# Reordering the steps of two state-space layers and an attention layer of one fused Trainium2 program

## The chip, the core and the metric

The program runs on one core of one Trainium2 chip. Five engines work side by side, each on its own queue and in the order of that queue: PE (TensorE, matrix products and transposes), DVE (VectorE), ACT (ScalarE), POOL (GpSimd) and SP (SyncE, which only issues transfers). They meet at semaphores alone. The metric is the time of one execution in device microseconds; the median of three runs counts.

## The reference, cut to what matters

Four layers follow each other on x of 8 sequences x 512 tokens x 256 features, all in float32: linear attention (layer 0), a state-space layer (layer 1), softmax attention with 16 heads (layer 2), and a second state-space layer (layer 3) whose tokens are permuted on the way in and back on the way out. All are modulated by a condition vector. A state-space layer computes, for one sequence:

```
h   = layernorm(x) * (1 + scale) + shift
xm, z = split(h @ W_in)                      # 512 channels each
u   = silu(causal_conv4(xm) + conv_b)
dtr, B, C = split(u @ W_x)                   # 64, 16, 16
dt  = softplus(dtr @ W_dt + b_dt)
s_t = s_{t-1} * exp(dt_t * A) + (dt_t * u_t) * B_t     # 512 x 16 states
y_t = sum_n s_t[:, n] * C_t[n] + u_t * D
out = x + gate * ((y * silu(z)) @ W_out)
```

The attention layer projects q, k and v, takes a softmax over 512 keys per head, normalises the result, and adds silu(...) @ W_out to its input.

## The kernel before, in words

**State-space layers (`mamba`, lines 579 to 1165).** The batch entry (one sequence) is the outer loop, `batches`: b = 0 alone, then a hardware loop of three turns over two batches each, then b = 7 alone. Inside a batch there are 64 units, `s = 4 n + j` for the state n (16) and the block j of 128 channels (4). For each unit

- ACT makes `dA = exp(dt * A)` (L837) into a ring of 8, and `dub`, the tokens of `dt * u` scaled by B, for the next n (L823), into two buffers;
- PE turns `dub` over into `ps_dbu` (L1150), a ring of 3 banks in PSUM;
- DVE scans along the tokens (L946, `TENSOR_TENSOR_SCAN`), which gives the state h;
- POOL multiplies h by C (L1012), and PE sums over n into `ps_y`: for odd n, DVE first adds two neighbours (L912, for three of four blocks, three units later), then PE adds the sum with an identity (L1137; L1133 and L1134 for the fourth block). The first such sum of each block also takes `u * D` (L1123). PE runs the sums seven units late.

Between the units stand the steps that prepare batch b + 1 (`prep_step` on each engine, by unit number): layer norm (statistics L867 and L872 on DVE, reciprocal root L752 on ACT, shift L877 on DVE, application L759 on ACT), turning (L1041), the eight input projections (L1052, four for xm, then four for z) whose results ACT copies out of the one PSUM bank `misc` (L769, L776), the convolution (L884 and three times L888 for each block), the two silus (L780, L782, with a load of their function table ahead and one behind), `u @ W_x` (L1062), and the softplus in pieces (L793 to L802, summed on DVE at L899). The steps that finish batch b - 1 (`post_step`, `out_proj`) stand there too. In layer 3, POOL gathers the rows of x by index for batch b + 1 ahead of unit 0 (L975, four DMAs) and the rows of the output of b - 1 ahead of unit 59 (L992, four DMAs), and adds them to the residual in one piece at unit 63 (L997).

**Attention layer (`softmax_attention`, lines 1184 to 1757).** A batch has 32 steps i. In each, PE writes two score matmuls for the exponentials (L1700) and two for the row maxima of work further ahead (L1693) into a ring of four banks; ACT takes the exponentials (L1579), DVE the maxima (L1414). Half of the steps also hold `times_v` (L1676). After eight steps the result of four heads is copied (L1421, `products_out`), turned (L1685, `turn`) and divided (L1431, `quotient`). The layer norms, q, k and v of later batches and the output projection of the batch before share two banks: `ps_x` for turning x, q, k (L1635) and v (L1643), `ps_o` for turning y (L1660) and the output (L1639, L1643). `take` makes PE wait until the last reader of a bank is through.

## Time and profile before

| | us |
|---|---|
| median of three runs (lowest, highest) | 3574.3 (3567.9, 3591.2) |
| the profiled execution, time | 3575.5 |
| its span | 3573.8 |
| busy in the span: PE, DVE, ACT, POOL | 2743.9 (77%), 2574.5 (72%), 2177.2 (61%), 1662.6 (47%) |
| layer 1: first scan to last | 438.1 to 1485.8 |
| layer 2: first exponential to last | 1620.9 to 2303.9 |
| layer 3: first scan to last | 2414.2 to 3526.5 |

A row of the profile names an engine, the line of the kernel, the operation and the tiles it writes and reads. Its time is the length of one instruction, or of several in a row where it ends in xN. Where the row has brackets, the engine stood idle before it for that long, and the name in them is what it waited for last. PEclk is TensorE's granted clock as a share of 2.4 GHz. Busy shares over the whole span mix four layers with different limits, so the windows of single batches tell more.

### The profile page before, as it was taken

The numbers are of one execution on the slowest core, as the hardware profiler recorded it, in microseconds if no ns is written. First come the engines' busy times: TensorE is split into PE (matmuls) and PEld (weight loads), VectorE is DVE, ScalarE is ACT, GpSimd is POOL, SyncE is SP. The second block draws the span as 40 slices with busy tenths as digits, with TensorE's granted clock in tenths as the row PEclk, the third lists the DMA queues.
The fourth block names the chain that finished last, engine by engine and source line by source line (L and its number), as shares of the span: only waits on it lengthen the run. The fifth ranks groups of instructions, "written<-read, shape, count | busy, mean of one in ns | idle before, by whom it ended". The sixth has DMA issues, their size and how long they took to land. (4 is left out here: it accounts for less than half of the span.)

```text
span 3573.8 us, 39139 instructions
## 1 busy us (share of the span) xinstructions
PE 2743.9 (77%) x11156; PEld 1451.4 (41%) x11156; DVE 2574.5 (72%) x3375; ACT 2177.2 (61%) x3550; POOL 1662.6 (47%) x1213
## 2 busy tenths in 40 slices
PE   5887487888878878748888888748787787877875
PEld 4555244445444445412333333214443444434443
DVE  2443288888888889767766677528888878888795
ACT  0333477877877878414554555537776776767773
POOL 0000167867767768720000000016776767768685
PEclk8899699999999999868988899968998899988998
DMA  2010101101111011143444444010101202111021
GB/s 85 24 35 18 63 24 49 54 26 56 39 41 56 31 49 49 49 78 52 70 66 73 72 72 66 19 63 25 49 32 48 68 25 67 37 55 55 25 72 43
DMA packets 104219, 176.92 MB, mean 50 GB/s; under 512 B 10741, under 2 KB 91421, under 8 KB 95166
## 3 DMA queue, kind: packets, MB, share of 16 engines
q1 hardware_dynamic: 99775, 161.69, 17.3%
q0 software_dynamic: 4224, 12.59, 1.0%
q8 instruction: 102, 1.67, 0.2%
q14 instruction: 118, 0.97, 0.1%
HBM read 139.70 MB, written 34.14 MB: 49 GB/s over the span
## 5 line engine op out<-in xcount | busy, mean ns | idle before, releaser
L1012 POOL TENSOR_TENSOR l_h<-l_h,l_c_all 128x512 f32<-128x512 f32 x1024 | 1437.7, 1420 | 559.0 <-DVE l_h L946 539.5
L946 DVE TENSOR_TENSOR_SCAN l_h<-l_dA,l_ps_dbu 128x512 f32<-128x512 f32 x1024 | 1211.6, 1207 | 307.6 <-PE l_ps_dbu L1150 167.3
L823 ACT ACTIVATE l_dub<-l_duT,l_b_tok 128x512 f32<-128x512 f32 x1024 | 725.8, 713 | 244.0 <-PE l_ps_dbu L1150 243.7
L1150 PE MATMUL l_ps_dbu<-ident,l_dub 128*128 128x128 f32 x4096 | 634.3, 289 | 264.2 <-DVE l_h L946 183.0
L1150 PEld LDWEIGHTS l_ps_dbu<-ident,l_dub 128*128 128x128 f32 x4096 | 495.1, 147 | 706.9 <-DVE l_h L946 388.3
L837 ACT ACTIVATE l_dA<-l_dt,l_a_neg 128x512 f32<-128x512 f32 x1024 | 727.9, 713 | 0.2
L1137 PE MATMUL l_ps_y<-l_h,ident 128*128 128x512 f32 x768 | 457.8, 682 | 81.7 <-DVE l_h L912 80.9
L1414 DVE TENSOR_REDUCE l_q_max<-l_ring 128x1 f32<-128x512 f32 x512 | 327.4, 683 | 192.9 <-PE l_ring L1693 191.6
L1579 ACT ACTIVATE l_probs<-l_ring 128x512 f32<-128x512 f32 x512 | 282.7, 596 | 300.7 <-PE l_ring L1700 298.9
L975 POOL DMA_INDIRECT l_x_in<-x_dram,l_idx_x x32 | 31.3, 978 | 805.7 <-DMA l_idx<-in_idx 792.6
L912 DVE TENSOR_TENSOR l_h<-l_h 128x512 f32<-128x512 f32 x384 | 351.5, 919 | 23.3 <-POOL l_h L1012 22.8
L1052 PE MATMUL l_misc<-l_modT,l_w_in 128*128 128x512 f32 x512 | 260.5, 634 | 20.2 <-ACT l_modT L764 9.5
L1693 PE MATMUL l_ring<-l_ks,l_qs 99*128 99x512 bf16 x512 | 216.4, 425 | 24.9 <-DVE l_q_max L1414 21.3
L1700 PE MATMUL l_ring<-l_qs,l_ks 102*128 102x512 bf16 x512 | 208.1, 411 | 18.2 <-DMA l_qs<-l_m_parts 6.4
L1137 PEld LDWEIGHTS l_ps_y<-l_h,ident 128*128 128x128 f32 x768 | 138.9, 214 | 189.9 <-DVE l_h L912 117.1
L888 DVE SCALAR_TENSOR_TENSOR l_work<-l_conv_in,vecs,l_work 128x512 f32<-128x512 f32 x192 | 181.7, 946 | 6.8
L979 POOL TENSOR_TENSOR l_conv_in<-l_dt,l_u 128x512 f32<-128x512 f32 x64 | 81.5, 1273 | 138.9 <-DVE l_dt L899 138.9
L1676 PE MATMUL l_ps_y<-l_probs,l_v 128*32 128x512 f32 x1024 | 143.0, 634 | 1.0 <-ACT l_probs L1579 1.0
L321 POOL DMA_DIRECT2D x_dram<-l_res x8 | 6.3, 786 | 293.2 <-DVE l_res L366 293.2
L1103 PE MATMUL l_misc<-l_w_out,l_y 128*128 128x256 f32 x512 | 120.8, 390 | 26.4 <-DVE l_og L919 24.9
L1052 PEld LDWEIGHTS l_misc<-l_modT,l_w_in 128*128 128x128 f32 x512 | 94.4, 205 | 109.0 <-issue 68.7
L1133 PE MATMUL l_ps_y<-l_h,ident 128*128 128x512 f32 x256 | 131.3, 595 | 0.0
(202 smaller groups left out, 3097.0 us busy)
## 6 DMA issues: line engine op xcount, KB each, us to landing
l_c_all<-c_rows_dram SPq DMA_DIRECT2D x64, 1024.0 KB, 4.7
l_res<-x_dram SPq DMA_DIRECT2D x24, 512.0 KB, 6.4
parts_dram<-l_parts SPq DMA_DIRECT2D x48, 256.0 KB, 2.7
l_qs<-parts_dram SPq DMA_DIRECT2D x48, 256.0 KB
l_ks<-parts_dram SPq DMA_DIRECT2D x48, 256.0 KB
l_x_in<-x_dram SPq DMA_DIRECT2D x16, 512.0 KB, 5.4
x_dram<-l_res SPq DMA_DIRECT2D x16, 512.0 KB, 3.2
su_cond_w<-in_cond_w SPq DMA_DIRECT2D x1, 5120.0 KB, 14.8
```

The lines of the kernel that those rows point to most:

```text
L823: return act.activation(dub[:, n % 2, t, :], duT[:, p, t, :], ACT.Copy, scale=b_tok[:, p, t, n:n + 1])
L837: act.activation(dA[:, s % DA_RING, :], dt[:, p, j, :], ACT.Exp, scale=a_neg[:, j * N + n:j * N + n + 1]).then_inc(da_ok, 1)
L912: dve.tensor_tensor(h[:, h_slot(s0), :], h[:, h_slot(s0), :], h[:, h_slot(s), :], ALU.add).then_inc(add_ok, 1)
L946: dve.tensor_tensor_scan(h[:, h_slot(s), :], dA[:, s % DA_RING, :], ps_dbu[:, dbu_slot(s), :], 0.0, ALU.mult, ALU.add).then_inc(scan_ok, 1)
L1012: pool.tensor_tensor(h[:, h_slot(s), :], h[:, h_slot(s), :], c_all[:, (n // C_GROUP) % 2, n % C_GROUP, :], ALU.mult).then_inc(hc_ok, 1)
L1052: last = pe.matmul(misc[:], w_in[:, k, e * P:(e + 1) * P], modT[:, k, :], start=(k == 0), stop=(k == DH - 1))
L1137: pe.matmul(ps_y[:, j, :], ident[:], h[:, h_slot(s0), :], start=False, stop=(n == N - 1), skip_group_check=True).then_inc(sum_ok, 1)
L1150: last = pe.transpose(ps_dbu[:, dbu_slot(s), t * P:(t + 1) * P], dub[:, n % 2, t, j * P:(j + 1) * P], ident[:])
L1414: dve.tensor_reduce(q_max[:, pair // 2, i, t:t + 1], ring[:, slot, :], AX.X, ALU.max).then_inc(smax_ok, 1)
L1579: act.activation(probs[:, pair % GH, half, t, :], ring[:, n % RING, :], ACT.Exp).then_inc(exp_ok, 1)
L1693: pe.matmul(ring[:, slot, :], qs[0:MAX_AT, p, hd, t * P:(t + 1) * P], ks[0:MAX_AT, p, hd, :], start=True, stop=True).then_inc(s_mm, 1)
L1700: pe.matmul(ring[:, slot, :], ks[:, p, hd, t * P:(t + 1) * P], qs[:, p, hd, :], start=True, stop=True).then_inc(exp_mm, 1)
```

## The change

It moves steps; nothing is computed otherwise. In the state-space layers:

- x is loaded (layer 1) or gathered (layer 3) two batches ahead, behind the turning of the batch before; the four gathers stand at units 18, 20, 22, 24, the gathers of y at 56 to 59, and the residual add is cut in two (units 62, 63);
- layer-norm statistics move from unit 7 to 0 and 1, the root from 8 to 3, the shift from 9 to 4, the application from 10 to 6, the turning from 12 and 14 to 9 and 11;
- the projections run xm, z, xm, z, ... at units 12, 14, ..., 26, where four of xm (15 to 21) and then four of z (23 to 29) stood;
- the convolution, four instructions in a row at units 18, 20, 22 and 24, becomes one instruction at each of units 15 to 30;
- `u @ W_x` is cut in two (units 34, 35), and the output projection in four (47, 48, 50, 51); what follows moves by one or two units;
- the hardware loop has two turns, and batches 5, 6 and 7 are written out.

In the attention layer, both kinds of work now alternate between `ps_o` and `ps_x` (`halves`), `turn` and `quotient` stand one step later than `products_out`, both silus stand at step 14, and the steps for batch b + 2 and the output are spread differently.

```diff
-            body(0, 0, False, True)
-            with eng.Fori(0, (B - 2) // 2) as pair:
-                body(pair * 2 + 1, 1, True, True)
-                body(pair * 2 + 2, 0, True, True)
-            body(B - 1, (B - 1) % 2, True, False)
+            body(0, 0, False, True, True)
+            with eng.Fori(0, 2) as two:
+                body(two * 2 + 1, 1, True, True, True)
+                body(two * 2 + 2, 0, True, True, True)
+            body(B - 3, (B - 3) % 2, True, True, True)
+            body(B - 2, (B - 2) % 2, True, True, False)
+            body(B - 1, (B - 1) % 2, True, False, False)
...
-                    if has_prep:
-                        load_x(b + 1)
                     if has_post:
                         res_load(b - 1)
                     c_load(b, p, 2)
+                    if has_far:
+                        load_x(b + 2)
...
-                    if s == 7: ln_stats(b)
-                    if s == 9: ln_shift(b)
-                    if s in (18, 20, 22, 24): conv(b, (s - 18) // 2)
+                    if s == 0: ln_stats_half(b)
+                    if s == 1: ln_stats(b)
+                    if s == 4: ln_shift(b)
+                    if 15 <= s < 15 + JB * TAPS: tap(b, (s - 15) // TAPS, (s - 15) % TAPS)
...
-                        if gathered and has_prep and s == 0: gather_x(b + 1)
-                        if gathered and has_post and s == 59: gather_y(b - 1, 1 - p)
-                        if gathered and has_post and s == 63: residual_rows(b - 1)
+                        if gathered and has_far:
+                            if s == 16: next_rows(b + 2)
+                            if s in (18, 20, 22, 24): gather_x(b + 2, (s - 18) // 2)
+                        if gathered and has_post:
+                            if s in (56, 57, 58, 59): gather_y(b - 1, 1 - p, s - 56)
+                            if s in (62, 63): residual_rows(b - 1, s - 62)
...
-                    if s in (12, 14): xn_half(b, (s - 12) // 2)
-                    if s in (15, 17, 19, 21): in_proj(b, (s - 15) // 2)
-                    if s in (23, 25, 27, 29): z_proj(b, (s - 23) // 2)
-                    if s == 34: x_proj(b, p)
+                    if s in (9, 11): xn_half(b, (s - 9) // 2)
+                    if s in (12, 16, 20, 24): in_proj(b, (s - 12) // 4)
+                    if s in (14, 18, 22, 26): z_proj(b, (s - 14) // 4)
+                    if s in (34, 35): x_proj(b, p, s - 34)
...
+        halves = (ps_o, ps_x)
...
-                    take(ps_x, rest_ok, b * 2 * DH + i * DH + g + 1)
+                    take(halves[g], rest_ok, b * 2 * DH + i * DH + g + 1)
...
-                            if i in (13, 14): silu_half(b - 1, i - 13)
+                            if i == 14:
+                                for h in range(DH):
+                                    silu_half(b - 1, h)
...
-                        if i in (14, 22, 30): turn(b, i // GU - 1)
-                        if has_post and i in (15, 16): project_out(b - 1, i - 15)
+                        if i in (15, 23, 31): turn(b, i // GU - 1)
+                        if has_post and i in (16, 17): project_out(b - 1, i - 16)
```

On DVE, around units 17 to 20 of a batch in layer 1 (here a scan is printed as SCALAR_TENSOR_TENSOR of `l_dA,l_ps_dbu`; L912 or L919 is the add of two states). Before:

```order
L912 TENSOR_TENSOR l_h<-l_h 128x512
L946 SCALAR_TENSOR_TENSOR l_h<-l_dA,l_ps_dbu 128x512
L884 TENSOR_SCALAR l_work<-l_conv_in,vecs 128x512
L888 SCALAR_TENSOR_TENSOR l_work<-l_conv_in,vecs,l_work 128x512 x3
L946 SCALAR_TENSOR_TENSOR l_h<-l_dA,l_ps_dbu 128x512 x2
L884 TENSOR_SCALAR l_work<-l_conv_in,vecs 128x512
```

Now, from unit 17:

```order
L954 SCALAR_TENSOR_TENSOR l_h<-l_dA,l_ps_dbu 128x512
L919 TENSOR_TENSOR l_h<-l_h 128x512
L896 SCALAR_TENSOR_TENSOR l_work<-l_conv_in,vecs,l_work 128x512
L954 SCALAR_TENSOR_TENSOR l_h<-l_dA,l_ps_dbu 128x512
L896 SCALAR_TENSOR_TENSOR l_work<-l_conv_in,vecs,l_work 128x512
L954 SCALAR_TENSOR_TENSOR l_h<-l_dA,l_ps_dbu 128x512
L892 TENSOR_SCALAR l_work<-l_conv_in,vecs 128x512
```

A block of four convolution instructions between two scans has become one behind every scan; in units 15 to 17 and 23 to 25 it stands behind a scan and an add.

On PE, units 13 and 14 of the same batch: before, two sums of states with their `u * D` and the second turning of x.

```order
L1123 MATMUL l_ps_y<-l_u,l_diag_d 128x512
L1137 MATMUL l_ps_y<-l_h,ident 128x512
L1150 MATMUL l_ps_dbu<-ident,l_dub 128x128 x4
L1123 MATMUL l_ps_y<-l_u,l_diag_d 128x512
L1133 MATMUL l_ps_y<-l_h,ident 128x512
L1134 MATMUL l_ps_y<-l_h,ident 128x512
L1150 MATMUL l_ps_dbu<-ident,l_dub 128x128 x4
L1041 MATMUL l_misc<-ident,l_x_in 128x128 x4
```

Now, from the end of unit 12 to unit 14:

```order
L1071 MATMUL l_misc<-l_modT,l_w_in 128x512 x2
L1149 MATMUL l_ps_y<-l_u,l_diag_d 128x512
L1163 MATMUL l_ps_y<-l_h,ident 128x512
L1176 MATMUL l_ps_dbu<-ident,l_dub 128x128 x4
L1149 MATMUL l_ps_y<-l_u,l_diag_d 128x512
L1159 MATMUL l_ps_y<-l_h,ident 128x512
L1160 MATMUL l_ps_y<-l_h,ident 128x512
L1176 MATMUL l_ps_dbu<-ident,l_dub 128x128 x4
L1071 MATMUL l_misc<-l_modT,l_w_in 128x512 x2
```

Of the four sums that carry `u * D` (units 11 to 14), one input projection now stands between the second and the third and one behind the fourth; before, the first stood at unit 15.

On ACT, steps 13 and 14 of the attention layer. Before:

```order
L1565 ACT_TABLE_LOAD
L1565 ACTIVATE l_hT<-l_ps_o,coef 128x512
L1576 REGISTER_ALU
L1579 ACT_TABLE_LOAD
L1579 ACTIVATE l_probs<-l_ring 128x512
```

The second silu follows with a load before it and one behind. Now:

```order
L1594 ACT_TABLE_LOAD
L1594 ACTIVATE l_hT<-l_ps_o,coef 128x512
L1593 REGISTER_ALU
L1594 ISA
L1594 ACTIVATE l_hT<-l_ps_x,coef 128x512
L1597 ACT_TABLE_LOAD
```

Two table loads a batch stand where four stood.

## Rows read from the trace of the kernel before

**Rows 1.** Windows, a batch each (layers 1, 3, 2): length, busy PE, PEld, DVE, ACT, POOL; PEclk, DMA.
```profile
705.50:842.60 137.10, 111.62 (x446) 63.39 (x447) 116.00 (x126) 103.59 (x167) 99.17 (x71) 0.93 0.13 45
2692.30:2839.40 147.10, 117.13 (x453) 65.23 (x453) 123.26 (x126) 105.48 (x169) 104.90 (x78) 0.88 0.15 49
1891.10:1984.50 93.40, 77.03 (x346) 29.15 (x344) 63.22 (x128) 47.84 (x84) 0.00 (x0) 0.90 0.38 70
```

**Rows 2.** Waits in the batch of layer 1: total us, times, longest.
```profile
DVE l_h L946 <- ACT l_dA L837: 10.0, 9, 3.5
DVE l_h L946 <- PE l_ps_dbu L1150: 9.5, 8, 3.1
```

**Rows 3.** Timeline of DVE, next batch: units 0, 7, 9, 13, 16, 33, 58 to 63.
```profile
842.59 1.21 DVE L946 TENSOR_TENSOR_SCAN l_h<-l_dA,l_ps_dbu 128x512 f32<-128x512 f32 x1
...
855.07 1.39 DVE L867 BATCH_NORM_STATS2 l_stats<-l_x_in 128x6 f32<-128x256 f32 x4
...
860.34 1.22 DVE L877 SCALAR_TENSOR_TENSOR l_shift<-l_moments,l_rstd 128x4 f32<-128x4 f32 x1
...
870.08 1.22 DVE L946 TENSOR_TENSOR_SCAN l_h<-l_dA,l_ps_dbu 128x512 f32<-128x512 f32 x1 [2.70 <-PE l_ps_dbu L1150]
...
876.96 1.22 DVE L946 TENSOR_TENSOR_SCAN l_h<-l_dA,l_ps_dbu 128x512 f32<-128x512 f32 x1 [0.76 <-PE l_ps_dbu L1150]
...
920.40 1.22 DVE L946 TENSOR_TENSOR_SCAN l_h<-l_dA,l_ps_dbu 128x512 f32<-128x512 f32 x1 [3.50 <-ACT l_dA L837]
...
968.79 6.97 DVE L946 TENSOR_TENSOR_SCAN l_h<-l_dA,l_ps_dbu 128x512 f32<-128x512 f32 x6
```

**Rows 4.** Timeline of PE in that batch: sums of states and input projections.
```profile
855.28 1.92 PE L1123 MATMUL l_ps_y<-l_u,l_diag_d 128*128 128x512 f32 x2
...
858.96 1.02 PE L1123 MATMUL l_ps_y<-l_u,l_diag_d 128*128 128x512 f32 x2
859.82 1.02 PE L1137 MATMUL l_ps_y<-l_h,ident 128*128 128x512 f32 x2
...
880.90 1.88 PE L1052 MATMUL l_misc<-l_modT,l_w_in 128*128 128x512 f32 x4
```

**Rows 5.** Timeline there: DVE and POOL instructions that both read two SBUF tiles.
```profile
858.04 0.67 DVE L912 TENSOR_TENSOR l_h<-l_h 128x512 f32<-128x512 f32 x1
858.21 3.34 POOL L1012 TENSOR_TENSOR l_h<-l_h,l_c_all 128x512 f32<-128x512 f32 x2 [1.93 <-DVE l_h L946]
...
882.08 3.21 DVE L888 SCALAR_TENSOR_TENSOR l_work<-l_conv_in,vecs,l_work 128x512 f32<-128x512 f32 x3
...
954.40 1.76 DVE L899 SCALAR_TENSOR_TENSOR l_dt<-l_conv_in,l_work 128x512 f32<-128x512 f32 x1
```

**Rows 6.** Timeline of ACT there: the first silu and its table load.
```profile
913.15 1.28 ACT L780 ACT_TABLE_LOAD   x1
914.45 1.91 ACT L780 ACTIVATE l_u<-l_work 128x2048 f32<-128x2048 f32 x1
```

**Rows 7.** Timeline of POOL and DVE across a batch boundary of layer 3.
```profile
3268.32 0.99 POOL L992 DMA_INDIRECT l_og<-y_even_dram,l_idx  x1
...
3275.63 7.06 DVE L912 TENSOR_TENSOR l_h<-l_h 128x512 f32<-128x512 f32 x2 [3.04 <-POOL l_h L1012]
...
3287.82 9.83 POOL L1012 TENSOR_TENSOR l_h<-l_h,l_c_all 128x512 f32<-128x512 f32 x8
...
3294.51 3.70 DVE L912 TENSOR_TENSOR l_h<-l_h 128x512 f32<-128x512 f32 x1
```

**Rows 8.** Waits of PE in one batch of the attention layer, 1793.5 to 1891.1.
```profile
PE l_ps_s L1685 <- DVE l_yT L1421: 6.5, 4, 1.6
...
PE l_ps_x L1635 <- DVE l_rest L1386: 1.8, 2, 0.9
PE l_ps_o L1660 <- ACT l_hT L1565: 1.6, 1, 1.6
PE l_ps_o L1639 <- DVE l_res L1454: 1.5, 1, 1.5
```

More of the change, by code:

```diff
@@ L1004, in body @@
                         if has_post:
-                            if not gathered and s in (50, 52): residual(b - 1, (s - 50) // 2)
+                            if not gathered and s in (51, 54): residual(b - 1, (s - 51) // 3)
                         n, j = s // JB, s % JB
@@ L1104, in out_proj @@
-                    last.then_inc(out_mm, 1)
+                    for k in range(JB):
+                        last = pe.matmul(misc[:, i * D:(i + 1) * D], y[:, k, t * P:(t + 1) * P], w_out[:, k, :], start=(k == 0), stop=(k == JB - 1),
+                                         skip_group_check=True)
+                    if i:
+                        last.then_inc(out_mm, 1)
                 def prep_step(s, b, p, after_post):
-                    if first(b) and s == 13:
+                    if first(b) and s == 10:
```

259 lines of the change are left out of this document (136 added, 123 removed).

## The prediction, made before the changed kernel ran

> **What bounds the kernel now.** The page's busy shares mix four layers, so I read windows that run from the first scan of a batch to the first of the next [rows 1]. In layer 1 a batch takes 137.1 us and DVE is busy for 116.0; in layer 3, 147.1 and 123.3; in the attention layer, 93.4 with PE busy for 77.0 and DVE for 63.2. So the state-space layers go by DVE and its idle time, and the attention layer by PE and its idle time. The wait view says who keeps DVE: ACT's dA for 10.0 us a batch and PE's ps_dbu for 9.5 [rows 2]. All seven batches that prepare a next one look alike, so what one gains is counted seven times a layer.
>
> The DVE timeline [rows 3] gives a batch its parts. Unit 0 starts at 842.59, unit 16 at 876.96, unit 33 at 920.40. A scan costs a step of some 1.13 us (six in 6.97, each overlapped a little by the next). In units 10 to 15 the scans wait for ACT and PE, 2.70 us the longest, because ACT did nothing between the statistics at unit 7 and the shift at unit 9 that it needed, and PE then came late to the four sums with u * D. The statistics row has no wait before it: x had long landed. So loading x earlier buys nothing in layer 1 but the right to start the norm earlier.
>
> One more resource has to be seen, since the change works on it most. DVE's add of two SBUF tiles and POOL's multiplication exclude each other [rows 5]: the add starts at 858.04 and takes 0.67, and two POOL instructions take 3.34 where eight in a row take 9.83, or 1.23 each [rows 7]. The softplus sum takes 1.76 where it stands behind an add, since POOL has meanwhile started. And at 3294.51 an add takes 3.70: it starts while POOL works off a run of eight and ends 0.56 after that run's end (3297.65). The Trainium skill (SBUF — State Buffer, section "SBUF: two separate sides") calls the shared port pair an exclusive lock which the first to start holds for its whole instruction. By that rule an add would wait for one instruction of 1.2 at most; the row shows it waiting for a run. The row decides, and it is what one rival below rests on.
>
> **State-space layers, units 0 to 15.** Before: 34.37 us. After, added up by units: unit 0 is 1.71 (scan and an add) + 0.80 (two of four statistics out of 1.39, rounded up), unit 1 is 1.13 + 1.04 (the other two, their wait and the aggregation), units 2 and 3 are 2.80, units 4 to 6 with a y product each 1.71, and the shift, now behind a scan and not behind an add, 0.15 for 1.22 [rows 3]. ACT gets two units of lead over DVE at each handover for one, so its waits do not reach DVE. Units 7 to 9 are 1.71 each with their adds, 10 to 12 are 1.13. That brings unit 13 to about 22.0. PE is later. Its first sum starts at about 14.5 and runs at the low clock (3.2 us from 855.28 to the next turning; the granted clock then rises, and a pair takes 0.86 by the starts of 858.96 and 859.82) [rows 4]. With the second sum, two turnings of 0.45, the projection newly put at unit 12 (1.9 at most, [rows 4]) and the third sum, unit 13 is ready at 24.8; the fourth sum (2.6) and the projection at unit 14 make 14 and 15 wait another 1.9 and 1.1. So 5.8 us of waits stay of 8.1, in the same place and now PE's alone; unit 15 starts at 30.0 and unit 16, with its scan, add and first tap (3.15), at 33.15. Gain 1.2 us.
>
> **Units 16 to 32.** Before: 43.44. A block of four convolution instructions cost 3.7 us; its three multiply-adds alone took 3.21 [rows 5]. After, each tap stands alone. Behind a scan alone it starts before POOL does, as the adds do, and costs 0.58: ten such units of 1.71 (one of them a little less). Behind a scan and an add it meets POOL, as the softplus sum does: 1.69 more, so units 16, 17, 24, 25 are 3.4 and 23 is 3.1. Sum for 16 to 30: 33.7; unit 31 is 1.7. At 32 both silus stand on ACT. Before, the table load began at 913.15 and the first silu at 914.45 [rows 6], and the next scan waited 3.50 [rows 3]. Now the silu waits for the last tap at unit 30; the load stands ahead of that wait. From the last tap: 1.9 + 1.8 + 1.3 + 0.7 = 5.7 to 5.9 until the next dA, less two units of 1.7 that DVE still has: 2.5 of wait, and unit 32 is 4.2. Sum 39.6, gain 3.8 us.
>
> **Units 33 to 63.** Of the four softplus sums two stood behind adds (47, 49); now one does (48): 1.1 us. The halved `u @ W_x`, the output projection in four and the moves by a unit or two I cost at nothing: PE waits for DVE there. If that cover is gone, it is ACT's 4.7 us of work per two units in the softplus that decides, as now.
>
> That is 6.1 us a batch. I charge 1.0 for the PE clock and for POOL lagging, neither of which I can place: 5.1 x 7 = **36 us in layer 1**. Bounds a batch: 0 to 9 (half of the 19.5 in [rows 2]).
>
> **Layer 3** has 10 us more a batch than layer 1 [rows 1], all of it POOL's. The four gathers of y (0.99 and a pause of 0.3, four times), the residual add, the index add and the four gathers of x make 12.5 us of POOL work; DVE's two adds at the boundary take 7.06 after waiting 3.04, and the add at unit 7 takes 3.70 for 0.67 [rows 7]. After, the gathers of y and the residual are the same work in the same region, where POOL has no slack: 7 us stay. Of the gathers of x, those at 18 and 24 fall into the pause that a tap behind an add makes; those at 20 and 22 cost 1.3 each, the index add nothing. So 9.6 for 10.5: **6.0 x 7 = 42 us**, bounds 0 to 11.
>
> **Attention layer.** PE waits 6.5 us a batch for the copy before `turn`, 1.8 for the rest of q and k, 1.6 for the first silu, 1.5 for the result [rows 8]: 11.4, all waits that the second bank or the later `turn` takes away. Five batches like that, one with 6.5, one with 9.4 and the last with 5.8 (same waits counted) give 79. New waits: the second turning of x now wants the bank that DVE frees at the same step, 0.8; and at steps 24 to 27 DVE holds the splits and the max parts together, as it did. I keep three quarters: **60 us**, bounds 25 and 90. Two table loads of 1.28 a batch go too; they lie inside this. The Trainium skill (ScalarE: Activation LUTs, section "What ACT_TABLE_LOAD costs") puts a switch of tables at about 2.66 us, load and drain. The trace has the next instruction 1.30 after the load begins [rows 6]. By the page the two loads would be worth another 2.7 us a batch, some 20 in all, a time near 3418.
>
> **Peeling.** One turn of the loop less in two layers; batches at the turn of the loop are up to 1.7 longer, so 0 to 5 us, taken as 0.
>
> **Sum.** The profiled execution took 3575.5 us, 1.2 over the median, so no correction is due. 3575.5 - 36 - 42 - 60 = **3438 us**.
>
> **Rivals.**
>
> - *Only the attention layer and little else gains.* PE's crowd at units 11 to 15 grows by the two projections (3.8 us) at the low clock, and the silu loses the lead of the block convolution. For it: 5.8 us of waits stay even in my count. Against: the projections at 27 and 29 are gone, and DVE, slower in units 15 to 17, lets PE catch up. Then 3575.5 - 60 - 10 = 3505, in 3475 to 3538.
> - *More.* PE keeps the high clock with fewer idle times, in attention all 79 and in the state-space layers 8 us a batch: 3575.5 - 79 - 8 x 14 = 3385.
> - *Slower: the taps lose the port.* Place: units 18 to 22 and 26 to 30. DVE's step there is 0.58 + 1.13, POOL's after DVE lets go is 1.13 by the rows of the adds. The margin is nothing, and the longest run of such units before was three. If POOL is 0.1 us late once, a tap starts behind it, and by the 3.70 row it waits for a run. With one instruction in progress and one queued, 2.3 us for each of ten taps, 14 batches: +322; if every second is hit, +161. From 3438 that is 3760 or 3600. The point from which it makes the kernel slower than before is a loss of 10 us a batch. By the page's rule of one instruction at most (1.1 a tap) it would end near 3590. The gathers at 20 and 22 make such lateness in layer 3, which speaks for it there; the three adds in a row, always 1.71 each, speak against.
> - *The change does not do what it says*: not so here; the order of the instructions is as described.
>
> **Chances.** A measurement of this kernel tells about 1% (36 us) from no change. Forecast, 3405 to 3475: 46%. Smaller gain, 3475 to 3538: 22%. More, below 3405: 17%. Nothing, 3538 to 3611: 8%. Slower by the port: 7%. So faster 0.85, same 0.08, slower 0.07. The range 3385 to 3525 leaves out the last two cases (15%) and a few per cent at the lower end.
>
> **What would show it.** Right: batches of layer 1 near 131 us, of layer 3 near 140, of attention near 83; taps of 0.7 behind scans and 1.8 behind adds; no wait of ACT's root reaching DVE; units 13 to 15 waiting for PE, unit 33 for ACT by some 2.5; PE's wait before `turn` gone. Wrong: taps of over 1 us behind a scan alone, a wait of DVE for POOL at units 20 to 23 of layer 3, or attention batches above 88, where DVE or ACT would have become the bound.

## The result, and the profile after

The changed kernel takes 3459.9 us (median of four runs, 3445.5 to 3462.9), the kernel before on the same chip 3571.7: a ratio of 0.9671 (95% interval 0.9646 to 0.9696), or 112 us less. The forecast was 3438 (3385 to 3525). The profiled executions have spans of 3573.8 and 3457.4 us, 116.4 apart, and each splits into these stretches (read from the starts and ends of the scans and exponentials):

| us | before | after | change | forecast |
|---|---|---|---|---|
| start to the first scan of layer 1 | 438.1 | 444.4 | +6.3 | 0 |
| layer 1, first scan to last | 1047.7 | 1024.8 | -22.9 | -36 |
| to the first exponential | 135.0 | 127.1 | -7.9 | 0 |
| attention, first exponential to last | 683.0 | 632.4 | -50.6 | -60 |
| to the first scan of layer 3 | 110.4 | 108.9 | -1.5 | 0 |
| layer 3, first scan to last | 1112.3 | 1074.0 | -38.3 | -42 |
| to the end | 47.3 | 45.8 | -1.5 | 0 |

Windows of one batch of layers 1, 3 and 2 after the change, with the columns of [rows 1]:

```profile
841.80:973.50 131.70, 110.65 (x461) 63.88 (x460) 116.11 (x124) 105.19 (x171) 101.43 (x70) 0.95 0.12 42
2750.70:2891.50 140.80, 112.38 (x453) 63.36 (x452) 123.05 (x126) 104.92 (x169) 109.33 (x79) 0.92 0.14 50
1842.80:1928.80 86.00, 75.49 (x343) 29.06 (x344) 61.69 (x127) 45.37 (x83) 0.00 (x0) 0.88 0.44 75
```

DVE is as busy as it was; only its idle time has gone. The view of waits for that batch of layer 1, against [rows 2]:

```profile
DVE l_h L954 <- PE l_ps_dbu L1176: 11.4, 9, 2.6
DVE l_h L954 <- ACT l_dA L840: 5.1, 5, 2.6
```

The waits for ACT are halved, those for PE have grown by 1.9. The DVE timeline of the batch shows where: units 12 to 14, a tap behind an add (unit 16), a tap behind a scan alone (unit 18), and scan 33, against [rows 3, 5].

```profile
866.39 1.22 DVE L954 TENSOR_TENSOR_SCAN l_h<-l_dA,l_ps_dbu 128x512 f32<-128x512 f32 x1 [2.63 <-PE l_ps_dbu L1176]
869.41 1.22 DVE L954 TENSOR_TENSOR_SCAN l_h<-l_dA,l_ps_dbu 128x512 f32<-128x512 f32 x1 [1.79 <-PE l_ps_dbu L1176]
871.56 1.22 DVE L954 TENSOR_TENSOR_SCAN l_h<-l_dA,l_ps_dbu 128x512 f32<-128x512 f32 x1 [0.93 <-PE l_ps_dbu L1176]
...
876.41 1.76 DVE L896 SCALAR_TENSOR_TENSOR l_work<-l_conv_in,vecs,l_work 128x512 f32<-128x512 f32 x1
...
882.62 0.72 DVE L896 SCALAR_TENSOR_TENSOR l_work<-l_conv_in,vecs,l_work 128x512 f32<-128x512 f32 x1
...
914.77 1.22 DVE L954 TENSOR_TENSOR_SCAN l_h<-l_dA,l_ps_dbu 128x512 f32<-128x512 f32 x1 [2.56 <-ACT l_dA L840]
```

The waits at 13 to 15, taps of 0.7 and 1.8, and the 2.5 before scan 33 are as forecast. What was not forecast is in units 48 to 52 of the same batch. PE first, then DVE: PE stands before the third quarter of the output projection (L1127) until DVE has gated the first half (L926).

```profile
946.85 1.99 PE L1127 MATMUL l_misc<-l_w_out,l_y 128*128 128x256 f32 x8 [2.65 <-DVE l_og L926]
```

```profile
944.44 1.75 DVE L906 SCALAR_TENSOR_TENSOR l_dt<-l_conv_in,l_work 128x512 f32<-128x512 f32 x1
946.11 0.68 DVE L926 TENSOR_TENSOR l_og<-l_misc,l_gate 128x512 f32<-128x512 f32 x1
...
951.90 0.69 DVE L926 TENSOR_TENSOR l_og<-l_misc,l_gate 128x512 f32<-128x512 f32 x1 [0.51 <-PE l_misc L1127]
953.28 2.52 DVE L954 TENSOR_TENSOR_SCAN l_h<-l_dA,l_ps_dbu 128x512 f32<-128x512 f32 x2 [0.69 <-PE l_ps_dbu L1176]
```

Unit 51 (950.17 to 953.28) takes 3.11 us where it took 1.11. The wait for the gate was there before too, ahead of the second half of the projection (all sixteen matmuls in one piece). PE before:

```profile
951.11 3.72 PE L1103 MATMUL l_misc<-l_w_out,l_y 128*128 128x256 f32 x16 [2.27 <-DVE l_og L919]
```

DVE then had 3.99 us of work of its own in unit 49 (952.69 to 956.68), with the softplus sum of 1.76 behind an add [rows 5]. Now that sum stands in unit 48, units 49 and 50 take 1.7 each, and what PE does behind its wait comes out.

Layer 3 has one more. POOL and then DVE around unit 21 of a batch:

```profile
2795.98 1.38 POOL L984 DMA_INDIRECT l_x_in<-x_dram,l_idx_x  x1 [0.15 <-issue]
2797.38 2.49 POOL L1025 TENSOR_TENSOR l_h<-l_h,l_c_all 128x512 f32<-128x512 f32 x2
```

```profile
2795.76 0.72 DVE L896 SCALAR_TENSOR_TENSOR l_work<-l_conv_in,vecs,l_work 128x512 f32<-128x512 f32 x1
...
2797.53 2.90 DVE L896 SCALAR_TENSOR_TENSOR l_work<-l_conv_in,vecs,l_work 128x512 f32<-128x512 f32 x1
```

The gather makes POOL late: its run of two starts 0.15 us before the tap and not behind it. The tap (one of the four convolution instructions of a block) takes 2.90 instead of 0.72 and ends 0.56 after that run (2799.87).

In the attention layer, the waits of PE in one batch, against [rows 8]:

```profile
PE l_ring L1725 <- DVE l_q_max L1441: 5.1, 3, 2.6
PE l_ring L1732 <- DMA l_qs<-l_m_parts: 3.7, 1, 3.7
PE l_ring L1732 <- ACT l_probs L1608: 2.1, 1, 2.1
PE l_ps_x L1657 <- DVE l_res L1481: 0.6, 1, 0.6
PE l_ps_s L1717 <- DVE l_yT L1448: 0.3, 1, 0.3
```

The waits before `turn` (6.5) and on the two banks (4.9) have become 0.9; 10.9 us of others, all on the ring, stand where there were 6.3.

To place the state-space changes, the mean of the seven batches that prepare a next one, by units (us, from the starts of the scans):

| units | layer 1 before | after | layer 3 before | after |
|---|---|---|---|---|
| 0 to 15 | 34.1 | 33.7 | 36.8 | 33.6 |
| 16 to 32 | 43.4 | 40.0 | 44.1 | 41.8 |
| 33 to 49 | 36.4 | 33.6 | 36.7 | 33.5 |
| 50 to 55 | 8.7 | 12.0 | 8.1 | 11.6 |
| 56 to 63 | 13.2 | 13.3 | 19.4 | 19.0 |

Work that moved across a border of this table moves time with it. Unit 15 now holds a tap and takes 3.14 us; in `blocks` below it holds none and takes 1.72, and there units 0 to 15 of layer 1 take 32.1 and 16 to 32 take 41.7. Units 33 to 55 together took 45.1 us in layer 1 and take 45.6; in layer 3, 44.9 and 45.1.

### The profile page after: what moved, and what is told of

Its sections match the earlier page's. It is cut to its first block and busy times, and to the rows that moved or that the text cites. A ratio compares the mean times of both kernels' runs of the same rounds, so it can differ in the third digit from the quotient of the medians.

```text
span 3457.4 us, 37654 instructions
## 1 busy us (share of the span) xinstructions
PE 2700.9 (78%) x11156; PEld 1445.5 (42%) x11156; DVE 2564.7 (74%) x3375; ACT 2152.1 (62%) x3536; POOL 1716.6 (50%) x1221
## 5 line engine op out<-in xcount | busy, mean ns | idle before, releaser
L1025 POOL TENSOR_TENSOR l_h<-l_h,l_c_all 128x512 f32<-128x512 f32 x1024 | 1482.4, 1458 | 466.8 <-DVE l_h L954 438.9
L1176 PE MATMUL l_ps_dbu<-ident,l_dub 128*128 128x128 f32 x4096 | 643.3, 290 | 259.0 <-DVE l_h L954 176.9
L1163 PE MATMUL l_ps_y<-l_h,ident 128*128 128x512 f32 x768 | 430.1, 644 | 51.8 <-DVE l_h L919 49.3
L919 DVE TENSOR_TENSOR l_h<-l_h 128x512 f32<-128x512 f32 x384 | 350.0, 915 | 11.6 <-POOL l_h L1025 11.4
L896 DVE SCALAR_TENSOR_TENSOR l_work<-l_conv_in,vecs,l_work 128x512 f32<-128x512 f32 x192 | 210.0, 1094 | 0.8
L1127 PE MATMUL l_misc<-l_w_out,l_y 128*128 128x256 f32 x512 | 129.7, 400 | 46.0 <-DVE l_og L926 35.4
L1159 PE MATMUL l_ps_y<-l_h,ident 128*128 128x512 f32 x256 | 133.7, 604 | 0.0
```

The lines of the kernel that those rows point to most:

```text
L896: dve.scalar_tensor_tensor(work[:, j, :], conv_in[:, j, k:k + T], vecs[:, wcol + k:wcol + k + 1], work[:, j, :], ALU.mult, ALU.add).then_i ...
L919: dve.tensor_tensor(h[:, h_slot(s0), :], h[:, h_slot(s0), :], h[:, h_slot(s), :], ALU.add).then_inc(add_ok, 1)
L1025: pool.tensor_tensor(h[:, h_slot(s), :], h[:, h_slot(s), :], c_all[:, (n // C_GROUP) % 2, n % C_GROUP, :], ALU.mult).then_inc(hc_ok, 1)
L1163: pe.matmul(ps_y[:, j, :], ident[:], h[:, h_slot(s0), :], start=False, stop=(n == N - 1), skip_group_check=True).then_inc(sum_ok, 1)
L1176: last = pe.transpose(ps_dbu[:, dbu_slot(s), t * P:(t + 1) * P], dub[:, n % 2, t, j * P:(j + 1) * P], ident[:])
```

## Experiments

Each ratio is to the kernel before on the same chip; the layers' times are from the profiled execution.

| | median us | ratio (interval) | layer 1 | attention | layer 3 |
|---|---|---|---|---|---|
| changed kernel | 3459.9 | 0.9671 (0.9646 to 0.9696) | 1024.8 | 632.4 | 1074.0 |
| att_only | 3520.9 | 0.9854 (0.9810 to 0.9898) | 1046.8 | 630.4 | 1116.5 |
| ssm_only | 3516.4 | 0.9840 (0.9793 to 0.9887) | 1024.7 | 681.4 | 1073.6 |
| out_late | 3436.6 | 0.9604 (0.9567 to 0.9641) | 1013.2 | 637.3 | 1062.0 |
| split29 | 3435.1 | 0.9618 (0.9585 to 0.9651) | 1024.7 | 613.4 | 1073.9 |
| blocks | 3472.5 | 0.9713 (0.9689 to 0.9737) | 1024.5 | 638.2 | 1087.8 |
| turn_early | 3508.4 | 0.9813 (0.9789 to 0.9838) | 1021.6 | 690.8 | 1073.9 |
| gath | 3446.7 | 0.9644 (0.9623 to 0.9665) | 1024.8 | 631.5 | 1063.7 |
| stackq | 3479.8 | 0.9724 (0.9702 to 0.9745) | 1024.7 | 656.2 | 1073.9 |
| turn_only | 3543.7 | 0.9891 (0.9861 to 0.9921) | 1046.8 | 652.8 | 1105.9 |
| blocks_z | 3467.2 | 0.9680 (0.9646 to 0.9713) | 1021.4 | 637.5 | 1087.8 |
| silus_apart | 3443.6 | 0.9611 (0.9583 to 0.9640) | 1024.7 | 618.5 | 1073.5 |
| best | 3392.2 | 0.9473 (0.9449 to 0.9497) | 1010.9 | 610.3 | 1045.3 |

Six kernels with the changed attention code untouched show what chance does to that layer: 630.4 to 638.2. Layer 1 with the same code repeats within 0.3 us in most, within 3.2 in all; layer 3 within 0.5 with the changed code, but 1105.9, 1112.3 and 1116.5 with the code of before, so the gain of layer 3 is known to be 32 to 43 us and no better.

**att_only**: the attention layer of the changed kernel in the kernel before.

```diff
 # layers 1 and 3: as before
-        # ps_x for x, q, k, v; ps_o for y and the output; turn at 6, 14, 22, 30
+        halves = (ps_o, ps_x)      # and the changed steps of layer 2
```

> The kernel before with the attention layer of the changed kernel; the state-space layers are as before. In the two profiles the stretch from the first to the last exponential went from 683.0 to 632.5 us (50.5), and the stretch from the last scan of layer 1 to the first exponential from 135.1 to 127.1 (8.0), of which it is not known to which edit it belongs. If the layers' gains simply add: 50 to 59 us less than before, a time of 3512 to 3522 against 3571.7. Rival, the layers are coupled through the granted clock, so that a layer's gain depends on what the others do: the stretch of the attention layer differs from 632.5 by over 5 us, or layer 1 and layer 3 (1047.7 and 1112.3 before) move by over 5 us though their code is unchanged.

The layer took 630.4, and the stretch ahead of it 127.6 (135.0 before). Both belong to this edit: 50.5 us by the medians, in the forecast range. The rival, a coupling through the clock, is not seen.

**ssm_only**: the other half.

```diff
+        # layers 1 and 3: as changed
         # layer 2: as before
```

> The kernel before with the state-space layers of the changed kernel; the attention layer is as before. If gains add: layer 1 from 1047.7 to about 1024.8, layer 3 from 1112.3 to about 1073.9, in all some 61 us, with 3 more from the stretches between layers, a time of 3503 to 3515. My forecast gave 78 for this part, which would be 3494. Rival, coupling through the clock: the stretch of the attention layer (683.0 before) moves by over 5 us. The start of layer 1 (438.1 before, 444.4 in the changed kernel, where three input projections ran at the low clock at 3.87 us instead of 2.07): if it comes from the steps of the state-space layer it shows here again, if it is chance of the clock it may not.

1024.7 and 1073.6: the times of both layers repeat to 0.4 us. The two halves give 50.5 and 55.1 less by the medians, together 106 of 112: within the intervals they add. There is no coupling to be seen in the layers' times. The later start of layer 1 is chance: it is 444.3 here, 443.6 in att_only, which has the old code, and 437.5 in gath, which has the new. In the changed kernel ACT's copies ahead of layer 1 show it:

```profile
383.60 0.60 ACT L772 ACTIVATE l_conv_in<-l_misc 128x512 f32<-128x512 f32 x1 [3.87 <-PE l_misc L1071]
388.07 0.60 ACT L779 ACTIVATE l_z<-l_misc 128x512 f32<-128x512 f32 x1 [3.87 <-PE l_misc L1071]
392.54 0.60 ACT L772 ACTIVATE l_conv_in<-l_misc 128x512 f32<-128x512 f32 x1 [3.87 <-PE l_misc L1071]
```

Three projections ran at the low level of the clock (granted 0.51 from 379 to 393), where in the kernel before ACT waited 2.07 for the second (granted 1.00 from 385 on).

**out_late**: second half of the output projection later.

```diff
-                        if has_post and s in (47, 48, 50, 51):
+                        if has_post and s in (47, 48, 52, 53):
-                    if s in (49, 52): out_gate(b, p, (s - 49) // 3)
+                    if s in (49, 54): out_gate(b, p, (s - 49) // 5)
-                            if not gathered and s in (51, 54): residual(...)
+                            if not gathered and s in (51, 56): residual(...)
```

> The changed kernel with the second half of the output projection two units later on PE (52 and 53 for 50 and 51), its gate on DVE at unit 54 for 52, its residual on POOL at 56 for 54. Theory: in the changed kernel PE stands at unit 50 for 2.65 us until DVE has gated the first half (behind its scan, add and softplus sum), with the transposes of units 51 to 53 queued behind it, and scans 51 to 53 pay: units 50 to 55 take 12.0 to 13.4 us where 8.7 stood. At unit 52 PE finds the gate of unit 49 done, since its ring lets it run three units ahead at most. Then units 50 to 55 fall by 2.5 to 4 us a batch, 14 batches, 35 to 55 us: 3405 to 3425 against 3459.9. In layer 3 the store of y comes two units later and the gathers at 56 may wait for it: up to 3 us a batch of that given back there. Rival, the loss at 50 to 53 is PE's four output projections of 1.9 us themselves, wherever they stand: 0, 3455 to 3465, with the same waits at units 53 to 55.

Units 50 to 55 fell to 10.4 and 10.0 (means of seven), 1.6 us a batch in both layers, half of what was expected, and the time of 3436.6 lies between the ranges of theory and rival. PE no longer waits for a gate in any batch that prepares a next one. DVE's wait for PE is smaller and has moved, as its timeline shows at unit 54:

```profile
945.13 2.33 DVE L954 TENSOR_TENSOR_SCAN l_h<-l_dA,l_ps_dbu 128x512 f32<-128x512 f32 x2 [1.51 <-PE l_ps_dbu L1176]
```

What is left stands behind PE's two quarters of 1.9 us, now among scans of 1.1 us. So the wait for the gate was one cause; that the projections cost so much wherever they stand is not so, as best shows: with them at 50 and 51 it takes 9.4. The store of y came in time in layer 3.

**split29**: the last split of q and k out of step 31.

```diff
-                            if i == 30: project(b + 2, 1, 1)
+                            if i == 28: project(b + 2, 1, 1)
-                            if i == 31: first_part(b + 2, 1, 1)
+                            if i == 29: first_part(b + 2, 1, 1)
-                            if i == 31: split(b + 2, 1, 1)
+                            if i == 29: split(b + 2, 1, 1)
```

> The changed kernel with the last q/k projection of batch b + 2 and its split at steps 28 and 29 of the attention layer instead of 30 and 31. Theory: at step 31 DVE does the quotient and this split in a row (2.9 us), the maxima behind them come late, PE waits 2.06 + 2.59 at the batch's start, the maxima of group 1 (step 2) come 3.5 us later after the batch's start than before, behind them the 2 MB of q and k of the next batch, which takes some 30 us, and at step 16 PE waits 3.74 for the transfer of maxima that is queued behind that. Moved, the two waits at the start shrink by some 3 us and the wait at step 16 by as much, less about 1 us at step 29, where DVE still works off the split and the parts of step 27: 3 to 6 us in six batches, 18 to 36 us: 3424 to 3442 against 3459.9. Rival, DVE's work is only shifted, and what it blocks at step 29 or 30 is as much: 3450 to 3465.

19 us less in the layer, within the expectation: DVE's crowd at the turn of a batch cost what it said (steps 28 to 31 fell by 7.8 us over the layer and step 1 by 11.0, together the whole gain). At step 16, though, the wait did not go. In this batch it changed its name, from 3.74 for the transfer of the maxima to this:

```profile
1869.31 0.61 PE L1732 MATMUL l_ring<-l_qs,l_ks 102*128 102x512 bf16 x1 [2.93 <-ACT l_probs L1608]
```

**stackq**: on split29, the transfers of q ahead of the maxima.

```diff
+                    if has_next:
+                        stack(b + 1, 1 - p, (0,))       # q
                     max_out(b, p, 1)
                     if has_next:
-                        stack(b + 1, 1 - p)
+                        stack(b + 1, 1 - p, (1,))       # k
```

> The previous experiment split29 (3435.1) with the transfers of q of the next batch issued at the batch's start, ahead of the maxima of group 1, and those of k behind them as before. In split29 the transfers run for some 30 us at about 122 GB/s and end about when step 16, which needs them, begins; PE still waits 9.8 + 7.9 us in the layer for them. If the transfers are what holds step 16 and 17, these go and the layer falls by 10 to 18 us: 3417 to 3425. Rival: at step 16 ACT's two silus with their two table loads (4.1 us in a row) end at the same time, PE waits for them instead (2.93 us in the batch where the transfer was in time), and the gain is 0 to 8: 3427 to 3435. Against it: the maxima of group 1 now stand behind 1 MB of q and may be late for step 8; then 3440 or more, with a wait for them at step 8.

43 us more: the clause against it held. The maxima of group 1 queue behind six transfers of 256 KB, and PE waits for them at step 8:

```profile
1866.50 0.38 PE L1735 MATMUL l_ring<-l_qs,l_ks 102*128 102x512 bf16 x1 [3.42 <-DMA l_qs<-l_m_parts]
...
1889.10 0.61 PE L1735 MATMUL l_ring<-l_qs,l_ks 102*128 102x512 bf16 x1 [2.92 <-ACT l_probs L1611]
```

At step 16 nothing was gained: the second row is the same wait for ACT as in split29, and all six batches have one of 2.92 to 2.99 there. So of two causes that ended together only one was removed.

**blocks**: the convolution in blocks of four again.

```diff
-                    if 15 <= s < 15 + JB * TAPS: tap(b, (s - 15) // TAPS, (s - 15) % TAPS)
+                    if s in (18, 22, 26, 30):
+                        for k in range(TAPS): tap(b, (s - 18) // 4, k)
```

> The changed kernel with the convolution of a block again as four instructions in a row, at units 18, 22, 26 and 30 (each the unit of the block's last tap), all else as in the changed kernel. My term for the taps says that four single taps behind scans cost 0.58 each, that those behind an add cost 1.69 more, and that a block of four costs 3.7. By the rows of the last batch, which has no taps, units 15 to 30 take 23.6 us without them; with four blocks 38.4, with the taps they took 36.8 to 37.1, so 1.4 us a batch, 13 or 14 batches: 3478 against 3459.9 (3470 to 3490). Where POOL catches up behind a block, DVE's wait at unit 23 (2.38 in the last batch) shrinks, and the loss with it. Rival one: PE with the projections of 1.9 us is what those units wait for, and the taps' form is worth nothing: 3455 to 3465. Rival two: with four instructions in a row POOL is locked out for 3.2 us, and its lateness comes out in waits of DVE at the next adds (23 to 25, 31): over 3490.

The time lies in the range of my theory, 3470 to 3490, but by luck, since the theory had 1.4 us a batch in both layers. In layer 1 nothing changed (1024.5 against 1024.8, and units 0 to 32 take the same within 0.2 us): four instructions in a row cost there what single taps cost. The whole loss, 13.8 us, is in layer 3, where the block and a later add meet the gathers. The DVE timeline has the add at unit 25:

```profile
2811.73 2.90 DVE L919 TENSOR_TENSOR l_h<-l_h 128x512 f32<-128x512 f32 x1
```

**blocks_z**: on blocks, the last z projection late again.

```diff
-                    if s in (14, 18, 22, 26): z_proj(b, (s - 14) // 4)
+                    if s in (14, 18, 22, 29): z_proj(b, (14, 18, 22, 29).index(s))
-                    if s in (16, 20, 24, 28): z_part(b, p, (s - 16) // 4)
+                    if s in (16, 20, 24, 31): z_part(b, p, (16, 20, 24, 31).index(s))
```

> The previous experiment blocks (four convolution instructions in a row at 18, 22, 26, 30; 3472.5, layer 1 1024.5 us) with the last z projection at unit 29 for 26 on PE and its copy at 31 for 28 on ACT, where the kernel before had it. blocks took as long in layer 1 as the changed kernel, so the taps are not what gained 3.3 us a batch in units 16 to 32. Theory: what gained it is that no projection stands among the plain scans of 1.1 us any more. In the kernel before, PE's projection of 1.9 at unit 27 or 29 makes DVE wait 1.38 at unit 29 and some 0.8 at 31, and ACT reaches the silus later, so that scan 33 waits 3.50 for dA where it now waits 2.5. Then this edit alone costs 1.5 to 3 us a batch in 7 batches of each layer: layers 1 and 3 together 20 to 40 us longer than in blocks, 3492 to 3512. Rival: DVE has slack there behind the blocks; 0 to 7 us, 3470 to 3480.

My theory fell: units 16 to 32 take what they took in blocks, 41.7 in layer 1 and 44.9 in layer 3. A late projection costs nothing where a block of DVE's stands behind it at unit 30.

**gath**: gathers of x earlier.

```diff
-                            if s == 16: next_rows(b + 2)
-                            if s in (18, 20, 22, 24): gather_x(b + 2, (s - 18) // 2)
+                            if s == 13: next_rows(b + 2)
+                            if s in (14, 15, 16, 17): gather_x(b + 2, s - 14)
```

> The changed kernel with the index add at unit 13 for 16 and the four gathers of x at units 14 to 17 for 18, 20, 22, 24, in layer 3 alone. In the changed kernel unit 21 takes 3.96 us in the six batches that gather and 1.77 in the one that does not. In units 13 to 17 DVE takes 3.0, 2.2, 3.1, 3.4, 3.4 us a unit, POOL 1.2. Theory: POOL's 1.1 us a gather fit there, unit 21 falls back to 1.77, 2.2 us in six batches: 13 us less, 3445 to 3449. Rival: at 16 and 17 an add, a tap and POOL already take turns at the shared port, and a gather makes POOL later by what the tap then waits: the 2.2 us come back there, 3457 to 3463.

Layer 3 fell by 10.3, and units 16 to 32 from 41.8 to 40.0, the value of layer 1. Here POOL has room, and no tap is late (POOL at units 14 and 15):

```profile
2765.64 1.02 POOL L984 DMA_INDIRECT l_x_in<-x_dram,l_idx_x  x1
2767.23 1.27 POOL L1025 TENSOR_TENSOR l_h<-l_h,l_c_all 128x512 f32<-128x512 f32 x1 [0.58 <-DVE l_h L954]
2768.65 1.01 POOL L984 DMA_INDIRECT l_x_in<-x_dram,l_idx_x  x1
```

**turn_early**: the late `turn` undone in the changed kernel.

```diff
-                        if has_post and i == 7: turn(b - 1, GROUPS - 1)
+                        if has_post and i == 6: turn(b - 1, GROUPS - 1)
-                        if i in (15, 23, 31): turn(b, i // GU - 1)
+                        if i in (14, 22, 30): turn(b, i // GU - 1)
                         # quotient likewise: 7, 15, 23, 31 for 8, 16, 24, 31
```

> The changed kernel with turn and quotient back at the step of products_out and the one behind it (turn at 6, 14, 22, 30, quotient at 7, 15, 23, 31), the rest of the attention layer as changed. My forecast had four waits of PE of 1.6 us a batch before the turn as its largest term of that layer. If they come back and what lies behind them on PE decides, the layer goes from 632.4 to 670 to 685 us, and the kernel to 3497 to 3512. Rival: PE has slack at those steps that the chain through the silus and the transfer of q and k at step 16 eats anyway; then 3460 to 3480, and the two banks and the spread of the steps made the gain.

690.8 for the layer: above my range for it (the kernel's 3508.4 lies in its own), and the loss is more than the layer's whole gain. The four waits are back, in the view of waits for one batch:

```profile
PE l_ps_s L1717 <- DVE l_yT L1448: 6.3, 4, 1.6
```

They are 6.3 us in this batch, and the layer lost 58.4 in eight. It lost them at steps 6 (23.0), 22 (15.9) and 30 (19.3); at step 14, where the two silus stand, seven of eight batches lost nothing for the same wait. Step 22 grew by 2.27, from 2.59 to 4.86. PE's last matmul into the ring starts at 1924.25 and takes 0.38, the wait is 1.62, and the turning takes 0.48 before the projection can start: 2.48 us, where the projection followed that matmul after 0.22.

```profile
1926.25 0.65 PE L1717 MATMUL l_ps_s<-ident,l_yT 128*128 128x128 f32 x4 [1.62 <-DVE l_yT L1448]
1926.73 1.88 PE L1667 MATMUL l_ps_o<-l_xnT,l_w 128*128 128x512 f32 x4
```

Step 6 grew by 3.8 in this batch, and there the clock came in. Behind a wait of 1.48, the projection of v takes 3.43 us, in a stretch with a granted clock of 0.55 (1878.3 to 1881.6):

```profile
1877.24 0.65 PE L1717 MATMUL l_ps_s<-ident,l_yT 128*128 128x128 f32 x4 [1.48 <-DVE l_yT L1448]
...
1878.35 3.43 PE L1675 MATMUL l_ps_o<-l_w,l_xnT 128*128 128x256 f32 x8
```

In the changed kernel it takes 1.99, at a granted clock of 1.00:

```profile
1858.63 1.99 PE L1675 MATMUL l_ps_o<-l_w,l_xnT 128*128 128x256 f32 x8
```

The first batch with this projection has 3.78 in both kernels; in the six behind it, it takes 2.8 to 3.7 here and always 1.99 there.

**turn_only**: the late `turn` alone in the kernel before.

```diff
-                        if has_post and i == 6: turn(b - 1, GROUPS - 1)
+                        if has_post and i == 7: turn(b - 1, GROUPS - 1)
-                        if i in (14, 22, 30): turn(b, i // GU - 1)
+                        if i in (15, 23, 31): turn(b, i // GU - 1)
                         # quotient, and the second norm, one step later
```

> The kernel before with one edit in the attention layer: turn and quotient one step later (and, behind the quotient at step 8, the statistics, root and application of the second norm one step later each); banks, silus and all else as before. In turn_early the layer took 690.8 us with all the other edits, over the 683.0 of the kernel before, and 632.4 with the late turn. If the late turn alone makes the gain, and the other edits are worth nothing or cost some us: 683.0 falls to 620 to 640, a time of 3510 to 3530 with no gain in the stretch before the layer. Rival: the late turn pays only together with the second bank and the spread of the steps, since otherwise PE's waits for the rest of q and k, the silu and the result take up what it frees: the layer stays at 645 to 670, 3535 to 3560.

652.8 for the layer and 3543.7 for the kernel: the rival's ranges, 30 us of gain in the layer. The waits for the rest of q and k (twice 0.89), the silu (1.62) and the result (2.35) are still there in a batch. So the parts of this layer do not add: alone, the late turn is worth 30 and all other edits -8; together 45 to 52.

**silus_apart**: on split29, the silus at 13 and 14.

```diff
-                            if i == 14:
-                                for h in range(DH):
-                                    silu_half(b - 1, h)
+                            if i in (13, 14): silu_half(b - 1, i - 13)
```

> The experiment split29 (3435.1, attention layer 613.4) with the two silus at steps 13 and 14, as before, which brings back two of four table loads in each of 8 batches. ACT's own time grows by 2 x 1.28 = 2.6 us a batch by the rows. At step 16 PE waits 2.9 us for ACT, behind the two silus and their loads. Theory one: the loads cost what the rows show, and all of it lies on the path: 7 or 8 x 2.6, the layer 18 to 21 us longer, 3453 to 3457. Theory two: apart, each block of load, silu and load is 3.3 us where one of 4.1 stands, and the four slots of the ring and the work between cover one of them: 5 to 12 us. Theory three: a switch costs more than the trace shows, 2.66 us (the Trainium skill, ScalarE: Activation LUTs, section What ACT_TABLE_LOAD costs); by it the layer would be about 40 us longer, 3475.

5 us more in the layer, at the edge of theory two and within chance, and the ratio is that of split29. That rules out the sums of theories one and three. ACT's timeline has the loads:

```profile
1868.67 1.28 ACT L1594 ACT_TABLE_LOAD   x1
1869.96 0.78 ACT L1594 ACTIVATE l_hT<-l_ps_o,coef 128x512 f32<-128x512 f32 x1
1870.76 1.28 ACT L1608 ACT_TABLE_LOAD   x1
1872.05 1.09 ACT L1608 ACTIVATE l_probs<-l_ring 128x512 f32<-128x512 f32 x2
```

Each load is 1.29 from its start to the next instruction. ACT has no slack there: in this batch it works without a pause through both steps (1867.56 to 1877.6), PE's waits for it in the layer rise from 16.4 to 36.7 us, and steps 13 and 14 together take 1.3 us a batch more, 9.4 in all. Elsewhere the layer got 4.3 shorter (step 17 by 5.8), and PE was busy for 547.8 us where it was for 558.3, at a granted clock of 0.94 for 0.93. Whether that follows from the edit or is chance is not shown; so two loads fewer a batch are worth some 5 to 9 us here.

**best**: split29, gath, and the first gate directly behind scan 48.

```diff
                     dve.tensor_tensor_scan(h[:, h_slot(s), :], ...)
+                        if has_post and s == 48: out_gate(b - 1, 1 - p, 0)
                         if s >= ADD_LAG:
                             add_states(b, s - ADD_LAG)
...
-                    if s in (49, 52): out_gate(b, p, (s - 49) // 3)
+                    if s == 52: out_gate(b, p, 1)
```

> The changed kernel with three edits: the last split of q and k at step 29 (split29, -24.8), the gathers of x at units 14 to 17 (gath, -13.2 by the medians, 10.3 in layer 3 by the traces), and, in place of out_late, the gate of the first half of the output put directly behind scan 48, ahead of the add and the softplus sum of that unit; output projections, second gate and residuals stay as in the changed kernel. If gains add and the gate's place was the whole cause of units 50 to 55 (12.0 to 13.4 us in the changed kernel, 10.8 in out_late): these fall to about 9.5, 3 us a batch, and the time is 3376 to 3390. Rival: PE's two projections of 1.9 us and its three sums and transposes of 1.3 between two gates are the bound there, as the wait of 2.15 at unit 53 in out_late suggests: 1.2 to 2 us a batch, 3392 to 3408. If gains do not add, over 3415.

A ratio of 0.9473 (0.9449 to 0.9497), below the changed kernel's 0.9671 (0.9646 to 0.9696). The kernel before took 3582.1 on that chip. The time of 3392.2 as it stands is the lower end of the rival's range; 0.9473 of the 3571.7 of the first comparison is 3383, in the theory's range. The units decide between the two. Units 50 to 55 fell to 9.4 in both layers, as the theory has it, since PE now waits 0.37 for the gate and not 2.65; split29 and gath, which have the gate where the changed kernel has it, left them at 11.6 to 12.0:

```profile
936.50 1.99 PE L1129 MATMUL l_misc<-l_w_out,l_y 128*128 128x256 f32 x8 [0.37 <-DVE l_og L926]
```

But in layer 1 units 56 to 63 grew from 13.3 to 14.2: POOL, without a pause since 939.67, is late, and the add at unit 57 takes 1.75 (unit 57 grew by 1.0):

```profile
952.70 1.75 DVE L919 TENSOR_TENSOR l_h<-l_h 128x512 f32<-128x512 f32 x1
```

## Why the prediction was right, and where not

The time lay in the range, 22 us above the forecast. The profiled spans differ by 116.4 us, 21.6 less than forecast: 13.1 of that in layer 1, 3.7 in layer 3, 1.5 in attention with the stretch before it, 6.3 in the start, less 3.0 in two stretches that I had at nothing. That all of it stayed so near is in part luck: layer 3 and attention each came out right by errors that cancel.

- **Layer 1, units 0 to 15**: 1.2 forecast, 0.4 measured as the mean of seven; in the batch shown, unit 16 starts after 32.9 us where I had 33.15. PE's waits are where I put them. Unit 0 was sized wrong: 3.04 for 2.51, since the add behind the two statistics meets POOL and takes 1.34.
- **Units 16 to 32**: 3.8 forecast, 3.4 measured, and every tap costs what I said, within 0.1 us. As an explanation it was still wrong to dwell on the taps: blocks shows their form worth nothing in layer 1. In blocks the same gain comes as 2.0 us in units 0 to 15 and 1.7 in 16 to 32; of the latter the wait for PE at unit 29 is 1.5 (2.57 us a unit before, 1.11 now) and the wait for the silus at unit 32 is 1.0 (5.26 and 4.28). The place of the projections was tried with blocks_z (worth nothing, as far as the last one goes). What is left is where DVE's convolution work stands: up to unit 30, beside PE's projections, instead of ending at 24 with three projections still to come. That fits both waits, but it is argued and not shown.
- **Units 33 to 63**, the step that failed: "The halved `u @ W_x`, the output projection in four and the moves by a unit or two I cost at nothing: PE waits for DVE there." I forecast 1.1 us a batch less from the softplus sum; units 33 to 55 together take 0.5 more in layer 1 and 0.3 more in layer 3, some 20 us over both layers, about as much as the forecast missed by. Within them 33 to 49 gained 2.8 and 3.2, and 50 to 55 lost 3.3 and 3.5. PE's idle time was no cover, because it is PE's lead of three units: the wait for the gate uses it up (2.27 before, 2.65 now), and the softplus sum that had given PE its time back in unit 49 had moved to 48. That the wait for the gate is the cause is shown by best, which takes 2.7 and 2.3 of it back, and by out_late; that the moved sum is what uncovered it is read from the rows and was not tried.
- **Layer 3**: 6.0 a batch forecast, 5.5 measured, by luck: I had 5.1 for what layer 1 gains too and 0.9 for layer 3 alone, and the runs show 3.3 and 2.2. The gathers at 20 and 22 were to cost 1.3 each; one of them costs 2.2, shown by the batch without gathers (unit 21: 1.77 for 3.96) and by gath.
- **Attention**: 60 forecast for the layer; 45 to 53 in the layer and 6 to 9 before it, in the prologue, which I had not counted. So of the 79 us of waits 57 to 67% stayed gained, and not three quarters, and the prologue made up for it. The prologue's part belongs to the banks and the spread of the steps, since turn_early keeps it and turn_only does not have it. The terms were not independent either: I summed PE's waits, and turn_only and turn_early show that one removed alone is worth half of what it is worth as the last (30 and 58 us).
- **Table loads**: 1.29 us each by the rows, and the two of a batch 5 to 9 us in the layer by silus_apart. By the Trainium skill's rule (ScalarE: Activation LUTs, section "What ACT_TABLE_LOAD costs") the time would have been near 3418, and silus_apart would have cost about 40 us, both by estimates from its 2.66 us. The rows and the run speak against it.
- **The rival of the port**: false for layer 1, where the lockstep at 1.77 us a unit held in every batch. True once a batch in layer 3, at the price it named (2.2 for 2.3 us), and for the reason that it gave: a gather makes POOL late, and the tap waits for a run, not for one instruction. The rule of one instruction (the Trainium skill, SBUF — State Buffer, section "SBUF: two separate sides") would have let that tap go after POOL's first multiplication, at about 1.8 us for 2.90 by an estimate from the page's rule (1.25 less 0.15, and 0.72); the row decides here.
- **Peeling**: no gain to be seen, and no run tried it alone. In layer 1 batches 5 and 6 (written out) take 133.6 and 132.6 where 3 and 4 (in the loop) take 131.7 and 132.8.

## What to carry to other kernels

An engine that waits is not thereby free: ask whether its waiting is the lead that hides the next delay, and cost every wait in its queue by what stands behind it and by what the other engine has to do meanwhile. When steps move by a unit, add up the stretch they leave and the one they enter together. Two waits that end together have to be removed together, and a wait for a transfer that sits in a shared queue is not cured by sending something else first. Where two engines share a port in lockstep, put the slower engine's extra work where the other is held up anyway.

## What the hardware showed that was not expected

- A wait of PE can cost more than its length by the clock behind it: after an idle time of 1.48 us the granted clock was 0.55, and eight matmuls took 3.43 us for 1.99 (turn_early, step 6). After one of 1.62 at step 22 it stayed at 1.00, and one at step 14 cost nothing.
- Code that is not touched still moves by chance: up to 7 us at the start of layer 1 (437.5 to 444.4), where the granted clock shows it, and 8 us in the attention layer (630.4 to 638.2), where PE is busy for 558 us in the run of gath and for 567 in that of blocks, at 0.92 and 0.90.
- An instruction of DVE that meets POOL takes 2.90 us in two different operations, an add and a tap, each time behind two multiplications of POOL.
